# Start addresses of three groups of matmul weights moved to 64 bytes behind a multiple of 512

## What is computed

```
n   = layernorm(x);  xp, z = split(n @ w_in)            # w_in 256 x 1024
xc  = silu(causal_conv4(xp) + conv_b)                   # 512 channels, 4 taps
h_t = 0.9 h_(t-1) + 0.1 (xc_t @ w_B);  ys_t = h_t @ w_C # 16 states
x   = x + (ys * silu(z)) @ w_out                        # w_out 512 x 256
s   = layernorm(x)[:, 0, :] @ Wr + br;  e1, e2 = top2(s)# one choice per sequence of 8 experts
x   = x + mean over e of (gelu(layernorm(x) @ W1[e] + b1[e]) @ W2[e] + b2[e])
```

## Time and profile before

| | |
|---|---|
| median of 3 runs | 509.06 us (508.75 to 509.20) |
| the profiled execution | 509.31 us, span 507.5 us, granted clock 1.0 |
| TensorE busy | 503.0 us (99%), 3026 matmuls |
| weight loads busy | 447.6 us (88%), 3026 |
| VectorE, ScalarE, GpSimd busy | 452.3 (89%), 400.7 (79%), 348.2 us (69%) |
| HBM read, written | 35.46 MB, 21.50 MB |

### The profile page before, as it was taken

The page is one execution under the profiler, slowest core; times in us unless marked ns, Lnnn a source line. Parts: engine busy times, 40 slices in busy tenths (PEclk is TensorE's granted clock), DMA queues, the critical chain, the costliest instruction groups (busy, mean ns, idle before and its releaser), DMA issues.

```text
span 507.5 us, 9839 instructions
## 1 busy us (share of the span) xinstructions
PE 503.0 (99%) x3026; PEld 447.6 (88%) x3026; DVE 452.3 (89%) x896; ACT 400.7 (79%) x692; POOL 348.2 (69%) x390
## 2 busy tenths in 40 slices
PE   8999999999999999999999999999999999999997
PEld 8889799898898989989899998989989899998997
DVE  6999899999998899989999899998999989996773
ACT  4986958878869788697887969779797887969454
POOL 4959597659693796928969197772977649673391
PEclk9999999999999999999999999999999999999999
DMA  8940005344251432606235170432604333130102
GB/s 266 292 174 12 32 0 173 119 131 162 74 182 37 165 124 83 206 17 193 79 124 165 42 223 24 165 124 86 203 40 143 106 125 125 51 115 0 43 3 83
DMA packets 53379, 57.28 MB, mean 113 GB/s; under 512 B 8682, under 2 KB 49642, under 8 KB 53226
## 3 DMA queue, kind: packets, MB, share of 16 engines
q1 hardware_dynamic: 51498, 56.67, 34.1%
q10 hardware_dynamic: 1856, 0.31, 0.3%
HBM read 35.46 MB, written 21.50 MB: 112 GB/s over the span
## 4 chain that ended last, share of the span: by engine, by line
PE 97%; DVE 1%; DMA 1%; issue 0%; DVEq 0%
PE blk L1291 16%; PE blk L1292 16%; PE blk L1296 16%; PE tok L1410 12%; PE tok L1408 12%; PE tok L1409 12%; PE turn L1449 3%; PE turn L1452 3%; PE blk L1471 3%; PE turn L1239 1%; PE tok L1291 1%; PE tok L1296 1%; PE tok L1292 1%; DMA x_mid<-in_L_attn_x 1%; DVE stats_t L914 0%; DVE normed L931 0%
## 5 line engine op out<-in xcount | busy, mean ns | idle before, releaser
L989 DVE SCALAR_TENSOR_TENSOR conv<-blk,tap_w,conv 128x512 f32<-128x512 f32 x192 | 130.1, 740 | 8.2 <-ACT conv L680 7.6
L485 POOL TENSOR_TENSOR y_lo<-gate,y_hi 128x512 fp32r<-128x512 f32 x57 | 72.2, 1299 | 36.6 <-ACT y_hi L608 36.5
L1291 PE MATMUL blk<-xn_hi,w_in_hi 128*128 128x512 f32 x228 | 89.5, 393 | 0.0
L1292 PE MATMUL blk<-xn_hi,w_in_lo 128*128 128x512 f32 x228 | 89.1, 391 | 0.0
L450 POOL TENSOR_TENSOR xc_lo<-conv,xc_hi 128x512 fp32r<-128x512 f32 x60 | 72.7, 1229 | 8.3 <-ACT xc_hi L608 8.1
L1408 PE MATMUL tok<-w_out_hi,y_hi 128*128 128x256 f32 x256 | 72.1, 282 | 0.0
L1410 PE MATMUL tok<-w_out_hi,y_lo 128*128 128x256 f32 x256 | 71.9, 281 | 0.0
L1409 PE MATMUL tok<-w_out_lo,y_hi 128*128 128x256 f32 x256 | 71.9, 281 | 0.0
L1296 PE MATMUL blk<-xn_lo,w_in_hi 128*128 128x512 f32 x228 | 70.3, 389 | 0.0
L1408 PE MATMUL tok<-w_hi,hid_hi 128*128 128x256 f32 x248 | 69.9, 282 | 0.0
L1410 PE MATMUL tok<-w_hi,hid_lo 128*128 128x256 f32 x248 | 69.7, 281 | 0.0
(11 more groups left out here) (189 smaller groups left out, 1321.7 us busy)
## 6 DMA issues: line engine op xcount, KB each, us to landing
spill<-normed SPq DMA_DIRECT2D x25, 512.0 KB, 2.8
normed<-spill SPq DMA_DIRECT2D x100, 128.0 KB, 2.8
out<-x_mid SPq DMA_DIRECT2D x30, 256.0 KB, 2.7
x_mid<-in_L_attn_x SPq DMA_DIRECT2D x29, 256.0 KB, 2.7
x_in<-in_L_attn_x SPq DMA_DIRECT2D x14, 512.0 KB, 4.3
w_all<-in_L_ffn_W SPq DMA_DIRECT2D x2, 2048.0 KB, 11.8
b_all<-in_L_ffn_b SPq DMA_DIRECT2D x1, 1024.0 KB, 13.1
gate<-in_L_attn_w_in SPq DMA_DIRECT2D x2, 256.0 KB, 4.5
```

The lines of the kernel that those rows point to most:

```text
L485: nc.gpsimd.tensor_tensor(y_lo[:, j, :], gate_of(o, j), y_hi[:, j, :].bitcast(F32), ALU.subtract).then_inc(y_lo_set, 1)
L989: nc.vector.scalar_tensor_tensor(cols, blk[j][:], tap_w[:, j, t:t + 1], cols, ALU.mult, ALU.add).then_inc(tap_added, 1)
L1291: mm(dst, whi(k), his(k), start=(k == 0), stop=False)
L1292: mm(dst, wlo(k), his(k), start=False, stop=False)
```

## The change

behind_columns, the unused 64 bytes, moves from behind c_mix to the front of b_mix. Two new tensors, last_hi and last_lo, 1024 bytes per partition each, follow c_mix. Being multiples of 512 they leave y_hi and what follows 64 bytes behind a multiple of 512. They get copies of the block j = 3 of the conv half of w_in_hi and w_in_lo, by two DMAs from SBUF to SBUF. From chunk 2 on, xp's block j = 3 takes its weights from the copies; in chunk 2 TensorE waits for them. The arithmetic is the same.

```diff
@@ -93,9 +93,10 @@
 
         w_in_hi, w_in_lo = sb("w_in_hi", [P, KD, 2 * DI], F32R), sb("w_in_lo", [P, KD, 2 * DI], F32R)
         w1_hi, w1_lo = sb("w1_hi", [P, TOP_K, KD * D], F32R), sb("w1_lo", [P, TOP_K, KD * D], F32R)
+        behind_columns = sb("behind_columns", [P, 16])
         b_mix = sb("b_mix", [P, JD, P], F32R)
         c_mix = sb("c_mix", [P, DI], F32R)
-        behind_columns = sb("behind_columns", [P, 16])
+        last_hi, last_lo = sb("last_hi", [P, KD, P], F32R), sb("last_lo", [P, KD, P], F32R)
         y_hi, y_lo = sb("y_hi", [P, JD, CH], F32R), sb("y_lo", [P, JD, CH], F32R)
         hid_hi, hid_lo = sb("hid_hi", [P, JF, CH], F32R), sb("hid_lo", [P, JF, CH], F32R)
 
@@ -110,6 +111,7 @@
         wout_loaded = sem("wout_loaded")
         taps_loaded = sem("taps_loaded")
         mix_loaded = sem("mix_loaded")
+        last_loaded = sem("last_loaded")
         late_loaded = sem("late_loaded")
         e_loaded = sem("e_loaded")
         x_loaded = sem("x_loaded")
@@ -368,6 +370,10 @@
                          W2.rearrange("e (k p) d -> p e k d", p=P)).then_inc(e_loaded, 16)
             sp.dma_start(b2_all[:], b2.rearrange("(o e) d -> o e d", o=1).broadcast_to([P, E, D])).then_inc(e_loaded, 16)
             fetch(3)
+            sp.wait_ge(w_hi_set, 2)
+            sp.wait_ge(z_out_lo_set, 1)
+            for dst, src in ((last_hi, w_in_hi), (last_lo, w_in_lo)):
+                sp.dma_start(dst[:].bitcast(F32), src[:, :, DI - P:DI].bitcast(F32)).then_inc(last_loaded, 16)
             fetch(4)
             spill(normed2, spill2, norm2_ready, tiles_normed(1, TT), spilled2)
             step(3, 1, 1)
@@ -1298,7 +1304,12 @@
 
             def in_proj(a, j, part, bank, sem_out):
                 cols = slice(part * DI + j * P, part * DI + (j + 1) * P)
-                project(bank, lambda k: w_in_hi[:, k, cols], lambda k: w_in_lo[:, k, cols],
+                his, los = w_in_hi[:, :, cols], w_in_lo[:, :, cols]
+                if part == 0 and j == JD - 1 and not (isinstance(a, int) and a < 2):
+                    his, los = last_hi, last_lo
+                    if isinstance(a, int) and a == 2:
+                        pe.wait_ge(last_loaded, 32)
+                project(bank, lambda k: his[:, k, :], lambda k: los[:, k, :],
                         lambda k: xn1(a)[0][:, k, :], lambda k: xn1(a)[1][:, k, :],
                         (t1_hi, t1_lo) if part == 0 and j == 0 else None, a, sem_out)
 
```

## The result

The changed kernel takes **510.46 us** (median of 8 runs, 510.15 to 511.67), the kernel before 509.06 us beside it (8 runs, 508.75 to 509.43): ratio 1.0031, 95% interval [1.0023, 1.0040]. By the medians it is slower by 1.4 us, where a gain of 0.6 was forecast. The profiled execution took 510.58 us.

What follows compares the result with a forecast made beforehand. TensorE's start-to-start matmul distance was taken to bound the kernel. Shifting 276 matmuls by 2.2 ns each saves 0.6 us, all else nothing: 508.4 us against the 509.06 median, range 503.0 to 509.6 (likeliest case 507.4 to 509.3).

Steps and rivals of the forecast that it cites:

- The frame: Whole kernel: TensorE is busy 99% of the span, so the distance between matmul starts sets the time; gains taken whole.
- signs that the prediction gave: Wrong if 256-column stretches move or TensorE waits near 39.7 us; eight of b_mix 1.79 us, above 1.84 for rival B.
- rival B: Shifted 512-column matmuls: switching between aligned and shifted weights costs 5 ns each, 1.4 us in all, to 510.4; chance 0.10.
- parts 3 and 4: Two copy DMAs on SP's queue, issued by 28.7 us, and TensorE's wait in chunk 2 near 39.7: both cost nothing.
- part 5: y_hi to hid_lo move by 2048 bytes, keeping their place behind a multiple of 512: put at nothing.
- part 2: Last conv block's copies, 84 matmuls; with b_mix and c_mix 276 of 512 columns, saving 2.2 ns each: 0.6 us.
- The bound: Each shifted 512-column matmul saves between nothing (or a loss) and 6.7 ns: 0 to 1.85 us for all.
- 276 x 5: All 276 shifted 512-column matmuls lie in a passage after a switch, 5 ns each: 1.4 us, to 510.4.
- Its counter-argument: Against rival B: at the switch to shifted weights behind b_mix, the first two steps take 0.24 us, usual pace at once.
- the chances: Faster than no change by over 1.02 us 0.43, within 0.47, slower 0.10; the 0.6 us gain itself 0.41.
- Rival A: 256-column stretches behind shifted matmuls flip to the 113.3 ns pace: 505.4 us with out_proj alone, 502.2 with all; chance 0.38.

Runs made afterwards that it cites:

- experiment 3: Changed kernel with copies, DMAs and wait, but copies, b_mix and c_mix all at a multiple of 512: 509.22 us against 509.07 for the kernel before, ratio 1.0003.
- experiment 1: Kernel before with only b_mix and c_mix shifted by 64 bytes, no copies: 509.89 us against 509.07, ratio 1.0017.
- experiment 2: Changed kernel with only the copies shifted by 64 bytes, b_mix and c_mix at a multiple: 509.71 us against 508.94 for the kernel before, ratio 1.0014.
- experiment 4: Kernel before with the weights of all 512-column matmuls shifted by 64 bytes, no copies: 514.96 us against 509.07, ratio 1.0114.
- experiment 5: TensorE-alone kernel, computation left out, operand offsets varied: weights at 0 and 64 bytes give 226.7 and 233.3 ns at 512 columns, 120.0 and 113.4 at 256.
- experiment 11: TensorE-alone kernel, matmuls of other widths put ahead of 48 with 256 columns at offset 64: 113.3 ns behind one of 256 columns, 117.7 behind 320.
- experiment 12: Kernel before with one 512-column product split in halves, one directly ahead of each out_proj and down from chunk 3: 506.22 us against 509.19, ratio 0.9936.
- experiment 9: TensorE-alone kernel with weights offsets 4 to 8 bytes apart: 256 columns 116.6 to 120.6 ns, 512 columns 226.7 to 233.3 ns.
- experiment 7: TensorE-alone kernel varying entry, order and offset of 48 matmuls with 256 columns: about 117.8 ns at offset 64 in every case, 116.6 at 480.

## Why the prediction was wrong

- **The frame held.** TensorE's start-to-start distance sets the time, and all of it reached the end: 1.27 us added to distances, 1.27 us added to the profiled execution. Of the signs that the prediction gave, no long 256-column stretch moved and no wait appeared near 39.7 us; the one for rival B came, with b_mix at 1.86 us, above 1.84.
- **The DMAs and the wait** (parts 3 and 4) cost nothing: experiment 3, ratio 1.0003. The issues took 0.73 and 0.64 us instead of 0.37, inside 20 us of slack. **The move of y to hid_lo** (part 5) cost nothing that shows (+0.06 us for y, -0.15 for hid).
- **The step that failed is in part 2**: "I take 2.2 ns, since the cost at a multiple is equal at both widths". The cost at a multiple is equal, 13 ns, but the shift acts on it with the other sign: -2.2 or -6.7 ns with 256 columns, +6.6 with 512 (experiments 1, 2, 4, 5). An equal sum at one offset was taken for an equal cause. The bound was wrong with it: "nothing saved (or a loss, below)" put a loss under rival B alone, at 0.10. In the sum the 0.6 us saved should have been 1.4 us lost: 212 x 6.6 ns, and nothing for the 64 of c_mix.
- **Rival B** had the direction and nearly the price: 276 x 5 = 1.4 us to 510.4 against 510.46. Its reason was wrong. Experiment 4 has no switch and costs most of all, and in experiment 5 the 233.3 ns last over 36 matmuls behind 12 of the same. And its 276 x 5 were 212 x 6.6, since the 64 of c_mix stand behind 256 columns anyway. That the two products agree is luck.
- **Its counter-argument** ("the first two steps take 0.24 us together" behind b_mix) spoke of 256-column matmuls again, as did every row at an offset of 64. There was no row with 512 columns and shifted weights, as the prediction says, and the chances should have been spread more evenly around zero for that.
- **Rival A** did not occur in the changed kernel: the long stretches behind shifted matmuls stay at 117.8 (experiments 1, 2 and the changed kernel); only 12 of down behind c_mix in the opening went to 113.8. That the pace hangs on the entry was right all the same. Experiments 11 and 12 show it by the width of the matmul ahead, and in experiment 4, with all wide weights shifted, a few stretches went over to 113.5 ns and gave 1.06 us back. Which ones do is not explained.
- By the Trainium skill, "TensorE: Matmul & The Clock Gate", Part 2, Step-by-step, weights and moving operand come through two independent read ports, and loading the next weights takes no read bandwidth from the running matmul. One would take from it that their addresses do not matter to each other. Experiment 5 does not agree with that: 226.7 and 233.3 ns for the same 512 columns, and 226.7 again when both are shifted. No run shows by what the two meet.

Open stays why 512 columns lose where 256 gain, what makes 112 or 256 columns ahead pick the fast pace and 128 or 320 the slow one, and whether at 256 columns the relative start decides as it does at 512. The tables say only when.

## What to carry to other kernels

A pace read at one tile shape is not one of another: with no row for the new shape, bound the cost on both sides of zero, and measure the offset by itself first. On a kernel that TensorE fills, place the weights by their start relative to the moving operand, each width for itself (here 512 columns at 0, 256 at 64 behind), and look at how a long stretch is entered: a half-width matmul directly ahead of each of 26 stretches was worth 3 us in all.

## What the runs showed of the hardware

- Start-to-start distance of matmuls with a new fp32r weights tile each, full clock: 512 columns 226.6 to 234.2 ns by the relative start of the operands (experiments 5 and 9); 256 columns 113.3 to 120.6 by the offset and by what stands ahead (experiments 5, 7, 9 and 11).
- 256 columns at offset 64 have two steady paces, 113.3 and 117.8 ns; a stretch of 48 keeps the one into which it falls within its first six (experiment 11).
- Behind 256 columns the first four to nine matmuls of 512 columns at a multiple take mostly 228 to 237 ns each instead of 226.7 (rows 8, experiment 7).
- The Trainium skill, "TensorE: Matmul & The Clock Gate", Part 2, Back-to-back issue gap, gives N / 2.4 + 2.5 ns for an isolated matmul, 215.8 for 512 columns, and about 131 ns at 512 columns for a stream in which each matmul has its weight load. The traces agree with neither: no stretch of 512 columns here came below 226 ns.
- A DMA from SBUF to SBUF of 128 KB with 512-byte pieces took SP 0.73 and 0.64 us to issue, against 0.37 for x_in.
